# First image in half pieces ahead of the weights, its normalisation on DVE and ACT, values written by two queues, scores in sets of three

## The reference

```python
x = x + attention(_gn(x))      # 12 heads of 32, window 7 x 7, and 16 register keys for all
x = x + experts(_gn(x))        # 4 experts, the top 2 of a softmax, hidden size 96 each
```

## Time and profile before

| | |
|---|---|
| median of 3 runs | 717.77 us (713.58 to 718.51) |
| profiled execution | 715.22 us, of which the span 713.3 |
| PE busy, PEld busy | 593.1 us (83%), 413.9 us (58%) |
| DVE busy | 474.6 us (67%) |
| ACT busy, POOL busy | 296.3 us (42%), 300.5 us (42%) |
| mean granted clock of PE | 0.962 |
| DMA | 95.93 MB, mean 134 GB/s |

### The profile page before, as it was taken

The page is one execution under the profiler, slowest core; times in us unless marked ns, Lnnn a source line. Parts: engine busy times, 40 slices in busy tenths (PEclk is TensorE's granted clock), DMA queues, the critical chain, the costliest instruction groups (busy, mean ns, idle before and its releaser), DMA issues.

```text
span 713.3 us, 22313 instructions
## 1 busy us (share of the span) xinstructions
PE 593.1 (83%) x9225; PEld 413.9 (58%) x9225; DVE 474.6 (67%) x1024; ACT 296.3 (42%) x586; POOL 300.5 (42%) x437
## 2 busy tenths in 40 slices
PE   0686899988997887987898878988777786799997
PEld 0433777667764765566765767557555443455554
DVE  3784566777976699774866768866797476652332
ACT  2343355315632377313552246323584226533231
POOL 4312789235221745318872532216454025621331
PEclk9997999999999999999999989999899898899999
DMA  8959751895359641694429772596520000001102
GB/s 322 277 152 219 203 131 46 215 252 149 92 126 238 187 114 45 164 263 135 123 72 256 209 174 59 123 240 177 152 57 2 1 33 34 34 34 67 66 36 99
DMA packets 130940, 95.93 MB, mean 134 GB/s; under 512 B 67340, under 2 KB 125384, under 8 KB 130072
## 3 DMA queue, kind: packets, MB, share of 16 engines
q1 hardware_dynamic: 121960, 78.72, 42.5%
q0 software_dynamic: 8880, 15.79, 7.4%
HBM read 58.11 MB, written 35.54 MB: 131 GB/s over the span
## 4 chain that ended last, share of the span: by engine, by line
PE 42%; DVE 20%; DMA 15%; ACT 7%; issue 7%; POOL 5%; SPq 3%; ACTq 0%; DVEq 0%; POOLq 0%
PE ps L904 25%; PE ps L1045 6%; DMA qscr<-QT 5%; DMA vscr<-VT 4%; DVE MX L523 4%; PE ps L1026 4%; PE ps L1002 4%; POOL vscr L339 3%; DMA KB<-kscr 2%; DVE GT_ L466 2%; DMA X<-in_x 2%; DVE ST L434 2%; DVE X L517 1%; ACT KB L734 1%; DVE KT L501 1%
## 5 line engine op out<-in xcount | busy, mean ns | idle before, releaser
L523 DVE TENSOR_REDUCE MX<-ps 128x2 f32<-128x456 f32 x216 | 124.4, 626 | 63.3 <-PE ps L1002 62.3
L904 PE MATMUL ps<-XH,WQ 128*128 128x384 f16 x810 | 151.6, 344 | 13.9 <-DVE XH L473 6.4
L904 PEld LDWEIGHTS ps<-XH,WQ 128*128 128x128 f16 x810 | 80.9, 102 | 76.7 <-issue 21.4
L787 ACT ACTIVATE PT<-ps 128x448 f32<-128x448 f32 (+1 forms) x162 | 79.0, 510 | 58.8 <-PE ps L1026 57.7
L1002 PE MATMUL ps<-KB,QS 120*32 120x228 f16 x1728 | 66.1, 276 | 31.9 <-DVE MX L523 9.9
L1026 PE MATMUL ps<-QS,KB 122*128 122x112 f16 (+1 forms) x864 | 65.6, 215 | 17.2 <-ACT VT L770 7.0
L339 POOL DMA_DIRECT2D vscr<-VT x108 | 57.2, 537 | 50.3 <-ACT VT L770 45.9
L409 POOL TENSOR_TENSOR OS<-QS,OS 128x384 f16<-128x384 f32 x36 | 32.3, 912 | 101.6 <-ACT OS L879 101.6
L904 PE MATMUL ps<-OS,WO 128*128 128x384 f16 x324 | 62.4, 343 | 13.3 <-DVE X L517 12.0
L332 POOL DMA_DIRECT2D qscr<-QT x36 | 26.3, 732 | 108.8 <-DVE QT L507 108.8
L1026 PEld LDWEIGHTS ps<-QS,KB 122*128 122x128 f16 x864 | 44.3, 100 | 38.4 <-ACT PT L787 13.0
(11 more groups left out here) (159 smaller groups left out, 978.7 us busy)
## 6 DMA issues: line engine op xcount, KB each, us to landing
KB<-kscr SPq DMA_DIRECT2D x108, 192.0 KB, 7.0
kscr<-KT SPq DMA_DIRECT2D x72, 192.0 KB, 2.5
VR<-vscr SPq DMA_DIRECT2D x216, 56.0 KB
QS<-qscr SPq DMA_DIRECT2D x108, 96.0 KB, 5.6
X<-in_x SPq DMA_DIRECT2D x6, 1152.0 KB, 18.9
qscr<-QT POOLq DMA_DIRECT2D x36, 192.0 KB, 5.1
vscr<-VT POOLq DMA_DIRECT2D x108, 64.0 KB, 2.3
out<-X SPq DMA_DIRECT2D x12, 576.0 KB, 3.3
```

The lines of the kernel that those rows point to most:

```text
L523: V.tensor_reduce(out=MX[:, s % 2, t, 2 * pair:2 * pair + 2], in_=ps[:, S_BANK(s, i), 0:2 * RUN].rearrange("p (h n) -> p h n", h=2), op=AL ...
L787: A(PTS[n % 4][:, 0:w], ps[:, ST_BANK(n), 0:w], ACT.Exp, scale=SCORE).then_inc(s_["exd"], 1)
L904: last = mm(bank, lhsT(a, k), rhs(b, k), start=(k == 0 and n == 0), stop=(finish and k == steps - 1 and n == 2))
```

## The change

The first image is loaded in six DMAs ahead of all weights, each half of a channel block with its own semaphore; the second image comes in six too. The tables (QS, KB) are loaded ahead of the weights of g = 1 and 2. In the first normalisation POOL makes no low half: DVE makes all three, and ACT makes the normalised float32 of block 2. PE runs 26 matmuls on zeroed memory first, and the group means leave out the two products of channel blocks that share no group. In stages 1 to 5 the values of odd tiles are written by SP's queue and those of even tiles by POOL's. PE's order becomes three units of scores, one tile of values, six times; in stage 0 three tiles of values and the value bias come ahead of all scores. The parameters of the next normalisation (stages 2 and 5) move from behind the queries to behind query tile 3. Banks of the turned maxima and of the scores from tile 3 on change places.

```diff
-POOL_K = ((0,), (0, 2), (0, 2), (0, 2))
+WARM = 26
+POOL_K = ((), (0, 2), (0, 2), (0, 2))
...
-        V_BANK = (2, 3, 2, 3, 2, 3)
+        V_BANK = lambda gi, s: 1 if gi and s == TILES - 1 else 2 + s % 2
...
-        S_BANK = lambda s, i: (0, 1, 4, 6, 5, 7)[i] if s < 3 else i % 2
+        S_BANK = lambda s, i: (0, 1, 4, 6, 5, 7)[i] if s < 3 else (i + 1) % 2
...                                  # SP
+            for c in range(KC):
+                for half in range(2):
+                    image_in(0, c, half)
             sp.dma_start(raw_g[0], wqkv[:, 0, :]).then_inc(w_in[0], 16)
-            for c in range(KC):
-                sp.dma_start(xs(0, c, 0, N), x[0, :, c, :]).then_inc(x_in[0][c], 16)
...
+            def values_out(gi, s):
+                sp.wait_ge(s_["v_sb"], 6 * gi + s + 1)
+                sp.wait_ge(s_["pv"], 36 * gi)
+                for b in range(KC):
+                    sp.dma_start(value_rows(s, b), VT[:, s % 2, b, :]).then_inc(s_["v_sp"], 16)
+
             def values_in(gi, s):
                 for t in {s, min(s + 1, TILES - 1)}:
-                    sp.wait_ge(v_out[t % 2], 144 * gi + 48 * (t // 2 + 1))
+                    if gi and t % 2:
+                        sp.wait_ge(s_["v_sp"], 144 * (gi - 1) + 48 * (t // 2 + 1))
+                    else:
+                        sp.wait_ge(v_out[t % 2], 144 * gi + 48 * (t // 2 + 1))
...
                 for s in (0, 1):
+                    if gi:
+                        values_out(gi, 2 * s + 1)
                     values_in(gi, s)
+                if gi:
+                    values_out(gi, 5)
...                                  # POOL
-                if gi == 0:
-                    for blk in range(STRIPS):
-                        if blk == 1:
-                            register_keys(gi)
-                        for k in POOL_K[0]:
-                            low_half(0, blk, k)
-                else:
-                    register_keys(gi)
+                register_keys(gi)
                 for s in range(TILES):
                     queries_out(gi, s)
+                if gi:
+                    register_values(gi)
                 for s in range(TILES):
-                    values_out(gi, s)
-                    if s == 1:
-                        register_values(gi)
-                    if s in (1, 3):
-                        maxima_in(gi, s // 2)
+                    if gi == 0 or s % 2 == 0:
+                        values_out(gi, s)
+                    if gi and s in (3, 5):
+                        maxima_in(gi, s // 4)
+                if gi == 0:
+                    register_values(gi)
+                    for s in (0, 1):
+                        maxima_in(gi, s)
...                                  # DVE
-                        for k in range(KC):
+                        for k in range(2):
                             normalised(0, a, k)
                         for k in range(KC):
-                            if k not in POOL_K[0]:
-                                low_half(0, a, k)
+                            low_half(0, a, k)
...                                  # ACT
             def values_out(gi, s):
                 act.wait_ge(s_["v_mm"], 6 * gi + s + 1)
-                if 144 * gi + 48 * (s // 2) > 0:
-                    act.wait_ge(v_out[s % 2], 144 * gi + 48 * (s // 2))
+                if gi and s % 2:
+                    act.wait_ge(v_out[1], 144)
+                    if 144 * (gi - 1) + 48 * (s // 2) > 0:
+                        act.wait_ge(s_["v_sp"], 144 * (gi - 1) + 48 * (s // 2))
+                else:
+                    if 144 * gi + 48 * (s // 2) > 0:
+                        act.wait_ge(v_out[s % 2], 144 * gi + 48 * (s // 2))
...
+                        if dve_lows(0, a) > 0:
+                            act.wait_ge(s_["gn_lo_v"], dve_lows(0, a))
+                        A(tmp_block(0, 2), x_block(0, a, 2), ACT.Identity, bias=cols["nb"][:, 2:3], scale=cols["rstd"][:, 2:3]).then_inc(s_["gn_ta"], 1)
+                        normalised(0, a, 2)
...
                 for s in range(TILES):
                     values_out(gi, s)
-                    if s in (1, 3):
-                        maxima_out(gi, s // 2)
+                    if gi and s in (2, 4):
+                        maxima_out(gi, s // 2 - 1)
+                if gi == 0:
+                    for s in (0, 1):
+                        maxima_out(gi, s)
...                                  # PE
+                    near = [k for k in range(KC) if abs(k - j) < 2]
...
+                if i == 0 and s == 2:
+                    pe.wait_ge(s_["t_ev"], 6 * gi + 1)
+                if i == 0 and s == 3:
+                    pe.wait_ge(s_["v_sb"], 6 * gi + 6)
...
                 if n < 2:
-                    pe.wait_ge(s_["v_sb"], 6 * gi + n + 5)
+                    pe.wait_ge(s_["v_sb"], 6 * gi + (5 if gi else 6))
...
+            pe.wait_ge(s_["pads"], 3)
+            for i in range(WARM):
+                mm(ps[0:LEAD, 6, 0:HEADS * LEAD], KB[0:96, 0, 0, 0:LEAD], KB[0:96, :, 0, 0:LEAD], start=True, stop=True)
...
-                for s in range(TILES):
-                    if s % 2 == 0:
-                        if s:
-                            maxima_turned(gi, s // 2 - 1)
-                        for i in range(6):
-                            scores(gi, s // 2, i)
-                    for b in range(KC):
-                        values(gi, s, b)
+                if gi == 0:
+                    for s in range(3):
+                        all_values(s)
+                    value_bias()
+                for k in range(6):
+                    three_scores(k)          # and maxima_turned(k // 2 - 1) for k in (3, 5)
+                    if gi:
+                        all_values(k)
+                    elif k < 3:
+                        all_values(3 + k)
```

More of the change, by code:

```diff
@@ L157, in tmp_block, with tmps @@
             return GT_[:, k, :].rearrange("p (s r) -> p s r", s=TILES) if n < 2 else GT_[:, k, :]
+        def tmps(n, blk, k):
+            return 2 * blk + k + 1 if n == 0 else (n - 1) * GN_STEPS + 2 * STRIPS + KC * blk + k + 1
         def pool_lows(n, blk):
@@ L170, in build @@
         s_ = {n: sem(n) for n in names}
-        x_in = [[sem(f"x_in{i}{c}") for c in range(KC)] for i in range(IMAGES)]
+        x_in = [[[sem(f"x_in{i}{c}{h}") for h in (0, 1)] for c in range(KC)] for i in range(IMAGES)]
         w_in = [sem(f"w_in{g}") for g in range(KC)]
@@ L213, in _, with image_in @@
         def _(sp):
+            def image_in(img, c, half):
+                sp.dma_start(xs(img, c, half * 3 * SN, 3 * SN), x[img, :, c, half * 3 * SN:(half + 1) * 3 * SN]).then_inc(x_in[img][c][half], 16)
+            for c in range(KC):
+                for half in range(2):
+                    image_in(0, c, half)
             sp.dma_start(raw_g[0], wqkv[:, 0, :]).then_inc(w_in[0], 16)
-            for c in range(KC):
-                sp.dma_start(xs(0, c, 0, N), x[0, :, c, :]).then_inc(x_in[0][c], 16)
+            sp.dma_start(QS[96:120, :, :], qtab.unsqueeze(1).broadcast_to([24, HEADS, N])).then_inc(s_["t_in"], 16)
+            for i in range(4):
+                sp.dma_start(KB[96:TROWS, :, i, :], ktab[1].unsqueeze(1).broadcast_to([26, HEADS, SLOTW])).then_inc(s_["t_in"], 16)
             for g in (1, 2):
@@ L219, in _ @@
             sp.dma_start(raw_o, wo).then_inc(s_["wo_in"], 16)
-            sp.dma_start(QS[96:120, :, :], qtab.unsqueeze(1).broadcast_to([24, HEADS, N])).then_inc(s_["t_in"], 16)
-            for i in range(4):
-                sp.dma_start(KB[96:TROWS, :, i, :], ktab[1].unsqueeze(1).broadcast_to([26, HEADS, SLOTW])).then_inc(s_["t_in"], 16)
             for c in range(KC):
-                sp.dma_start(xs(1, c, 0, N), x[1, :, c, :]).then_inc(x_in[1][c], 16)
+                for half in range(2):
+                    image_in(1, c, half)
             def keys_out(gi, a):
@@ L275, in _ @@
                 if gi == STAGES - 1:
-                    for i in range(2):
-                        sp.wait_ge(v_out[i], 144 * STAGES)
+                    sp.wait_ge(v_out[0], 144 * STAGES)
+                    sp.wait_ge(s_["v_sp"], 144 * (STAGES - 1))
                     for src, dst in ((fc2, f2raw), (rw, rwraw)):
@@ L624, in _ @@
                             if gi == 1 and s == 0 and a < 3:
-                                dve.wait_ge(x_in[1][a], 16)
+                                for half in range(2):
+                                    dve.wait_ge(x_in[1][a][half], 16)
                             last = block_statistics(1 if gi == 1 else 0, a % 3, j)
@@ L910, in group_means @@
                 for j in range(KC):
-                    for k in range(KC):
-                        last = mm(ps[:, bank, 2 * j:2 * j + 2], G[:, k, j * P:(j + 1) * P], mv[:, k, :], start=(k == 0), stop=(k == KC - 1))
+                    near = [k for k in range(KC) if abs(k - j) < 2]
+                    for k in near:
```

(17 more changed lines are left out.)

69 lines of the change are left out of this document (40 added, 29 removed).

## The result

The changed kernel takes 743.33 us (median of 4 runs, 740.26 to 748.80); the kernel before, on the same chip, 717.44. The ratio is 1.038 [1.030, 1.046]: 3.8% slower. I predicted 726 us with a range of 707 to 735. The direction was right, the size was not: the loss of 26 us is three times the forecast 8 us. The profiled execution took 748.80 us (span 747.0), the slowest of its four, and the one of the kernel before lay 2 us under its median, so some 8 us of what the two traces differ by are these two runs'.

The account below looks back on a forecast made before the run. The prediction took tile 5's value copy, waiting on value-write landings, to set each stage, with further waits in the head and at queries. 715.22 - 5.0 + 12.9 + 3.2 = 726.3, so 726 us, range 707 to 735.

Parts of the forecast that it names:

- -5.0 for head and stage 0: Start to stage 0's end: earlier image, group means and strips save 5.0 us, between 3.5 and 8.
- +12.9: Stages 1 to 5: tile 5's copy ends later by 3.8, 2.6, 0.8, 3.7 and 2.0 us, +12.9 in sum.
- +3.2: Stages 1 and 4: PE idles with tile 5 late and its clock falls, 1.6 us a fall, bounds 0 and +5.
- the warmed clock: Head: the clock raised by 26 warming matmuls was expected lost before the group means, and counted as nothing.
- Together 12.3: Stages 1 to 5: SP's path from the end of its query issues to tile 5's copy takes 12.3 us.
- The part for tile 1: SP's list, stages 1 to 5: two issues ahead of the third (1.3) plus the landing (2.5), 3.8 us.
- +31: Stages 1 to 5: upper bound of the sum, with landings of 5.2 and 3.2 us and a 15.9 us path.
- whatever moves the end of tile 5's copy moves the stage: Stage 1: PE runs nearly without gaps after tile 5's copy, so that copy's end sets the stage.
- SP's lateness spreads: Rival, stages: tile 5's write and the second value loads push key loads 0.8 us a stage; 735 to 745; chance 0.08.
- The clause for stage 0: Stage 0: the first maxima land near 84.1, 4.3 us before ACT's first exp at 88.44.
- by itself nothing: Scores in threes: PE's work between first scores and key_scores stays 13.6 us, so the new order costs nothing.
- The rule: Value writes: a second issuer saves only sequencer time, some 1 us a stage; by it alone the sum would be 705.

Follow-up runs that it names:

- e3: The changed kernel with SP's writes of value tiles 1 and 3 both ahead of all its value loads; 743.80 us, 1.041 of the kernel before.
- e4: The kernel before with the new head alone (image first in half pieces, tables earlier, warming matmuls, fewer group means); 718.37 us, 1.006 of before.
- e9: The kernel before with scores in threes alone, including banks, value bias and place of the parameters; 722.15 us, 1.015 of before.
- e14: The kernel before with scores in threes, first maxima among stage 0's value tiles and a third value slot, POOL writing all values; 712.44 us, 0.998.
- e11: The kernel before with a third slot for value tiles, the SUMT buffer; 708.06 us, 0.990 of before.
- e7: The changed kernel with all value writes on POOL and stage 0's first maxima copied among the value tiles; 717.59 us, 1.012 of before.
- e12: The changed kernel, SP still writing odd value tiles, with a third value slot (SUMT); 737.90 us, 1.030 of before.
- e13: The changed kernel with all value writes on POOL, first maxima among stage 0's value tiles, and a third value slot; 710.10 us, 0.989 of before.
- e15: The changed kernel with a third value slot, ACT's queue writing tiles 1 and 3 and POOL tile 5 in stages 1 to 5; 715.11 us, 0.997.

## Why the prediction failed, step by step

**The account.** The terms of the sum were -5.0 for head and stage 0, +12.9 and +3.2 for stages 1 to 5: +11.1, which became +8 because they were added to a profiled execution 2.6 us under the median. The traces have +1.4, +25.7 (A +18.6, B +7.1) and 6.6 outside of all terms. So 6.4 us of the miss are the head's, 9.6 the stages', and 6.6 belong to neither.

**Right.** That this is slower, and by which mechanism: SP's list, with ACT idle before tile 5 on a vscr landing and PE idle in front of the first exps. Six loads were taken at 4.2 us and took 4.20. The group means took 3.12 us for the 3.1 forecast; the warmed clock was lost, as expected.

**The failed step: "Together 12.3", as the price of SP's list.** Two terms in it were wrong.
- The size. Measured is 13.5 as a mean. The part for tile 1 was taken at 3.8 from the kscr rows; SP's first value load starts 6.0, 4.4, 4.9, 3.4 and 4.5 us behind the query issues, 4.6 as a mean. In stage 1 the landing took 4.06, between the 2.5 I took and the upper bound of 5.2. Stage 3 has slower issues: 2.74 and 2.94 us for the two writes, 5.06 for the six loads between them. The sum is +18.6 for +12.9, inside the upper bound (+31; its own terms add up to 15.7 us a stage and +30).
- What it left out. I followed the list to tile 5's copy and stopped. Behind it stand the value loads and the keys of tiles 4 and 5. In the changed kernel B grew by 7.1 us. In e3, where tile 5's copy was made early, A fell by 11 and B rose by 13, with the waits for keys. So the copy of tile 5 does not decide the stage by itself, as the prediction had it ("whatever moves the end of tile 5's copy moves the stage"); SP's list behind it does too. I had that as a rival, "SP's lateness spreads", 735 to 745, at 0.08, and 743 is in its range, in part by luck: it priced the spread at 0.8 us a stage, where B has 1.4, took the rest from longer landings, and still counted the head's -5.0.

**Head, -5.0.** With the first exp of stage 0 at 89.77 for 88.44, it was +1.3. The prediction's own working gave -4.3, and the sum took -5.0. The landing was taken from the bytes moved away, 3.5 us with the statistics; aggregation began 1.1 earlier in the changed kernel and 2.4 in e4. The clause for stage 0, first maxima landed near 84.1, counted POOL's issues and took the landings for hidden. ACT's copies of tiles 2 to 5 wait 5.06, 0.50, 3.28 and 1.37 us. The second copy of maxima waits for scores that wait for the first.

**Scores in threes, "by itself nothing".** PE's work between first scores and `key_scores` is indeed the same, but I compared PE's list only. On ACT's, the first maxima moved from behind tile 1, with no wait for a landing, to behind tile 2, with the longest; on POOL's, their writes moved behind value tiles 3 and 5, and `key_scores` waits for them. Price of the whole order alone: 1.5% (e9), and with a third slot 0.8% (e14 against e11).

**Clock, +3.2.** The mean granted clock fell from 0.962 to 0.925. With two levels, 1 and 0.5, that is 54 and 112 us at the lower one. At most half of the 58 more is lost, and only where PE is the limit. In e4, 0.943 goes with +0.6%. So the clock is a part of each wait's price, and no run measures the +3.2 by itself.

**The rule.** The Trainium skill, "DMA: Bandwidth & Descriptors", section "Issuing engines are not separate DMA queues", leaves a second issuer its sequencer time alone. The runs agree: with the third slot and the threes, writes on ACT and POOL (0.997) are not faster than on POOL alone (0.989, with stage 0 as in e7 too). The gain of about 5 us that I drew from it for this change did not exist, since the sequencer that was given the work was not free.

## What to carry to other kernels

Before a DMA moves to another engine's queue, read that queue's list to its end: the transfer's issue and each landing that the issuer waits for are added to everything behind it, also to loads that come much later. If a wait for a landing stands in the way, a further buffer takes it away (1 to 2% here), where a second queue or another order only moved it. Ask first who else uses that buffer: the same slot was free in e11 and cost PE up to 13.9 us in e12, because there the write out of it stood last on SP's list. When an order of work is changed on one engine, compare what now stands ahead of each copy and each write on the engines that serve it. And when a stage is cut into stretches, see that they leave no gap: A and B together say that e13's stages are as short as e11's, and the 6.9 us between them say that they are not.

## What the hardware showed unexpectedly

Halving the pieces of the first image did not bring the last one earlier: 2.6 and 2.5 us apart for 576 KB each, where 1152 KB came 4.21 us apart. The DMA engines were busy all that time (share 1.03 from 12 to 16 us). In e4, with the same head, the last piece reached DVE at 15.75 and not 17.07; whether two runs of one kernel differ as much, no run shows.

The same 64 KB writes took 4.8 us to land (median of 30) from ACT's queue in e15, and 2.4 (median of 45) from SP's in the changed kernel. The time did not follow these landings.
